# A macaron network of four layers on one core: grouped projections with joined weights, paired tiles and paired key chunks, and a later load of the second group

## What is computed

```python
def global_latent_attn(x, wq, w_kv_down, w_k_up, w_v_up, wo):
    q = split_heads(x @ wq, H)
    latent = x @ w_kv_down
    k = split_heads(latent @ w_k_up, KVH)
    v = split_heads(latent @ w_v_up, KVH)
    q, k = (rope(q, BASE_G), rope(k, BASE_G))
    q, k = (qk_norm(q), qk_norm(k))
    ...
x = x + global_latent_attn(rmsnorm(x, norm1_w), g_wq, g_kv_down, g_k_up, g_v_up, g_wo)
x = x + local_gqa_attn(rmsnorm(x, norm2_w), l_wq, l_wk, l_wv, l_wo)
```

## Time and profile before

| | us |
|---|---|
| median of 3 runs (1966.89 to 1970.33) | 1969.22 |
| the profiled execution | 1968.03 |
| its span, first to last instruction | 1966.3 |
| TensorE busy in it (86%) | 1696.1 |
| VectorE busy (49%) | 954.9 |
| ScalarE busy (41%) | 814.5 |

### The profile page before, as it was taken

One profiled execution on the slowest core, in us unless ns is written; L12 is line 12 of the kernel. 1 busy time (PEld: TensorE's weight loads), 2 busy tenths in 40 slices (PEclk: granted clock), 3 DMA queues, 4 the chain that ended last, 5 costly groups with the idle time before them and its releaser, 6 DMA issues. The chain is left out here.

```text
span 1966.3 us, 25234 instructions
## 1 busy us (share of the span) xinstructions
PE 1696.1 (86%) x8834; PEld 911.8 (46%) x8882; DVE 954.9 (49%) x2236; ACT 814.5 (41%) x1325; POOL 306.1 (16%) x443
## 2 busy tenths in 40 slices
PE   7688896499998988799889999999869985789998
PEld 2334564244443556344444454666623333454665
DVE  5755236687775333511351013445643348774445
ACT  5354133256667323222132124221378864654221
POOL 1102322122233423100210004000100001014000
PEclk9888998699999899899989999999679996889999
DMA  3623104400100310000000002553231103403553
GB/s 81 255 60 133 53 22 104 119 26 26 50 26 2 143 45 28 16 0 0 1 0 0 0 21 66 132 116 83 47 89 31 31 4 81 125 30 78 120 127 86
DMA packets 55383, 120.90 MB, mean 61 GB/s; under 512 B 7767, under 2 KB 34007, under 8 KB 50467
## 3 DMA queue, kind: packets, MB, share of 16 engines
q1 hardware_dynamic: 52796, 114.31, 21.9%
q0 software_dynamic: 2432, 5.00, 0.8%
q10 hardware_dynamic: 39, 0.07, 0.0%
HBM read 86.14 MB, written 19.96 MB: 54 GB/s over the span
## 5 line engine op out<-in xcount | busy, mean ns | idle before, releaser
L970 PE MATMUL psum<-f_h,w 128*128 128x512 f32 (+1 forms) x512 | 223.4, 594 | 8.6 <-ACT f_h L941 6.2
L1754 DVE TENSOR_REDUCE a_most<-psum 128x1 f32<-128x512 f32 (+3 forms) x304 | 182.0, 656 | 46.2 <-PE psum L1604 34.2
L1716 ACT ACTIVATE a_probs<-psum 128x512 f32<-128x512 f32 (+1 forms) x304 | 155.3, 578 | 94.8 <-PE psum L1634 62.6
L2550 ACT ACTIVATE t_silu<-psum 128x512 f32<-128x512 f32 x136 | 81.2, 597 | 241.1 <-PE psum L2608 240.0
L2625 PEld LDWEIGHTS psum<-t_slot,t_hid 128*128 128x128 f32 x1024 | 132.0, 191 | 55.9 <-issue 49.7
L970 PEld LDWEIGHTS psum<-f_h,w 128*128 128x128 f32 x512 | 96.0, 190 | 131.7 <-issue 118.9
L2002 ACT ACTIVATE ga_probs<-psum 128x1024 f32<-128x1024 f32 (+2 forms) x160 | 138.3, 952 | 23.6 <-PE psum L1918 23.4
L2721 DVE TENSOR_TENSOR t_prod<-t_silu,psum 128x512 f32<-128x512 f32 x104 | 71.6, 688 | 137.4 <-ACT t_silu L2550 137.4
L2625 PE MATMUL psum<-t_slot,t_hid 128*128 128x128 f32 x1024 | 134.5, 276 | 2.9 <-DVE t_hid L2712 2.9
L2608 PE MATMUL psum<-xnT,t_slot 128*128 128x512 f32 x256 | 131.5, 595 | 3.1 <-ACT t_silu L2550 3.1
L2613 PE MATMUL psum<-xnT,t_slot 128*128 128x512 f32 x256 | 130.7, 592 | 0.0
(11 more groups left out here) (379 smaller groups left out, 2859.1 us busy)
## 6 DMA issues: line engine op xcount, KB each, us to landing
t_spread<-factors SPq DMA_DIRECT2D x64, 512.0 KB, 6.4
m_experts<-experts_dram SPq DMA_DIRECT2D x14, 768.0 KB, 10.3
c_halves<-xnT SPq DMA_DIRECT2D x48, 128.0 KB, 2.3
t_slot<-experts_dram SPq DMA_DIRECT2D x32, 192.0 KB, 5.3
a_qs<-scratch_q SPq DMA_DIRECT2D x16, 288.0 KB
a_ks<-scratch_k SPq DMA_DIRECT2D x24, 192.0 KB
ga_qs<-scratch_q SPq DMA_DIRECT2D x16, 288.0 KB
la_qs<-scratch_q SPq DMA_DIRECT2D x16, 288.0 KB
```

The lines of the kernel that those rows point to most:

```text
L970: ins = pe.matmul(core.psum[:, HID[n % 2], :], w(name, i * HT + j), src, start=(i == 0), stop=(i == HT - 1))
L1716: act.activation(probs[:, (n * BLOCKS + b) % PROBS, h0:h0 + heads, 0:wide], src, ACT.Exp, scale=SCALE).then_inc(probs_ready, 1)
L1754: v.tensor_reduce(most[:, row, h0:h0 + heads, qt % KPH], src, AX.X, ALU.max).then_inc(max_read, 1)
```

## The change

- `Split` counts queries and keys with semaphores of their own. With `pair=2` (kinds "g" and "l") keys are cut into parts once for two chunks: the even chunk's keys are turned to PSUM rows 0 to 31, the odd chunk's to rows 32 to 63, by a matmul with the identity at a tile position, and the three copies and two subtractions of the keys run on 64 rows after the odd chunk alone; two DMAs store them.
- "g": the compressing weights are turned and multiplied by the up weights once, on TensorE, and ScalarE copies query weights and products into one 128 x 352 tile `joined`. `down` and `compressed` go; a tile's projection is one matmul, as in "l".
- ScalarE writes the cosines and sines out for all tiles at the start of the stage (`turn_by`, `table`). A product instruction then covers two tiles and both tables, 128 x 640 out of two PSUM banks. ScalarE copies the values of two tiles at a time.
- `project(0)` moves ahead of the turning of chunks 2 and 3. `heads` holds all chunks.
- The squares are written head by head, so that the head sums read adjacent elements. The Newton step has three instructions.
- `ahead` is 1 in all three attentions: group 1 is loaded in the attention stage.

```diff
-        for i, transfers in enumerate((self.PARTS, 1)):
-            for odd in range(2):
-                sp.wait_ge(self.spilled[i][odd], 16 * transfers * chunks // 2)
+        for odd in range(2):
+            sp.wait_ge(self.spilled[0][odd], 16 * self.PARTS * chunks // 2)
+            steps = (chunks // self.pair + 1 - odd) // 2
+            if steps:
+                sp.wait_ge(self.spilled[1][odd], 16 * self.pair * steps)
...
+        step, odd = divmod(c, self.pair)
+        if odd == self.pair - 1:
+            sp.wait_ge(self.part_ready[1], self.parted(step, self.PARTS - 1))
+            rows = self.rows[1] // self.pair
+            for k in range(self.pair):
+                b, at = divmod((step * self.pair + k) * CH, T)
+                dst = self.scratch[1][:, b, :, at:at + CH].rearrange("p r t -> r p t")
+                sp.dma_start(dst, self.parts[1][k * rows:(k + 1) * rows, :, step % 2, :]).then_inc(self.spilled[1][step % 2], 16)
...
+            if kind == "g":
+                pe.transpose(core.psum[0:LATENT, DOWN_BANK, 0:P], w("g_down"), core.c("ident")).then_inc(down_pe, 1)
+                pe.wait_ge(down_ready, 1)
+                a = L3_COLS["g_k"][0]
+                pe.matmul(core.psum[:, UP_BANK, 0:3 * VW], down_turned[:, :], w5[0:LATENT, a:a + 3 * VW], start=True, stop=True).then_inc(up_pe, 1)
 
             def project(c):
+                pe.wait_ge(ln.xnT_ready, c + 1)
                 for t in range(TPC * c, TPC * (c + 1)):
                     if t >= TPC:
-                        pe.wait_ge(cos_step, 2 * (t - TPC + 1))
-                        pe.wait_ge(v_ready, t - TPC + 1)
...
+                        pe.wait_ge(turned_by, (t - TPC) // 2 + 1)
+                        pe.wait_ge(v_ready, (t - TPC) // 2 + 1)
+                    pe.matmul(core.psum[:, QKV_BANK[t % TPC], 0:WIDE], core.xnT[:, t * P:(t + 1) * P], weights, start=True, stop=True).then_inc(qkv_pe, 1)
...
+                for t in range(TPC):
+                    ins = pe.matmul(core.psum[rows, T_BANK[1], t * P:(t + 1) * P], heads[:, c, t, D:QK], core.c("ident"), start=True, stop=True, tile_position=(0, odd * VW))
+                if odd == PAIR - 1:
+                    ins.then_inc(sp_.heads_pe[1], 1)
 
             ln.tensor(pe, 0)
             ln.tensor(pe, 1)
-            down(0)
+            if kind == "g":
+                pe.wait_ge(joined_ready, 4)
+            project(0)
             ln.tensor(pe, 2)
-            down(1)
             ln.tensor(pe, 3)
-            project(0)
-            down(2)
-            down(3)
             project(1)
...
+            act.activation(turn_by[:, :, :, :].rearrange("p f k (d h) -> p (f k d) h", h=GROUP), by_tile, ACT.Copy).then_inc(turn_by_ready, 1)
+            act.wait_ge(turn_by_ready, 1)
+            for f in range(2):
+                dst = table[:, :, f, :].rearrange("p k (g r) -> p k g r", r=HD * GROUP)
+                act.activation(dst, turn_by[:, f, :, :].unsqueeze(2).broadcast_to([P, TILES, HN // GROUP, HD * GROUP]), ACT.Copy).then_inc(table_ready, 1)
...
-                act.activation(square[:, :, :], heads[:, c % 2, :, :], ACT.Square).then_inc(squared, 1)
+                dst = square[:, :, :, :].rearrange("p t (g h) d -> p (t g) d h", h=GROUP)
+                act.activation(dst, heads[:, c, :, :].rearrange("p t (g d h) -> p (t g) d h", d=HD, h=GROUP), ACT.Square).then_inc(squared, 1)
...
+                v.tensor_tensor(both[:, 2 * k:2 * k + 2, :, :].rearrange("p t f q -> p t (f q)"), core.psum[:, bank:bank + 2, 0:2 * QK],
+                                table[:, at:at + 2, :, :].rearrange("p t f q -> p t (f q)"), ALU.mult).then_inc(turned_by, 1)
...
-                s.chain(v.tensor_reduce(per_head(mean[:, :, :]), by_head(square[:, :, :]), AX.X, ALU.add))
+                s.chain(v.tensor_reduce(mean[:, :, :], square[:, :, :, :], AX.X, ALU.add))
...
-            stacks = Stacks(core, actx, "a1_", sems["a1_"], scratch, (P, P), [GROUP, T], 3, 2)
+            stacks = Stacks(core, actx, "a1_", sems["a1_"], scratch, (P, P), [GROUP, T], 3, 1)
...
-                stacks = Stacks(core, actx, tag, sems[tag], scratch3, (P, 4 * HD), [T], ring, 2)
+                stacks = Stacks(core, actx, tag, sems[tag], scratch3, (P, 2 * 4 * HD), [T], ring, 1, pair=2)
```

240 lines of the change are left out of this document (109 added, 131 removed).

## The result

The changed kernel took 1944.17 us (median of 4 runs, 1938.66 to 1948.27) beside 1969.78 for the kernel before on the same chip: ratio 0.9875, 95% interval 0.9853 to 0.9897. On another chip it took 1940.07 beside 1971.87, ratio 0.9846 (0.9813 to 0.9880). The gain is 25 to 32 us. The forecast was 1937 with a range of 1928 to 1948.

What follows compares the result with a forecast made beforehand. It took TensorE to set the pace in the global projection, VectorE in the local one, with SyncE late at each projection's end. Gains by stage, less load costs, summed to 32.5 us off 1969.2: forecast 1937, range 1928 to 1948.

Steps and rivals of the forecast that it cites:

- second layer, projection's end: Second layer's projection: without group 1's load, chunk 3's parts are issued earlier; gain 7 us, bounds 5 and 9.
- The walk over the two projections: Global and local projections: stepping through four engines' lists gave rounds of 23.7 us (global) and 22.1 us (local).
- most of it lies under the head of the stage: Guarded attention: group 1's moved load costs between 0 and 5.0 us, taken as 1 because the stage's head covers most.
- the loads come late: Rival: second layer's first maxima wait the full 5 us, band attention's second group 3; 1943.5 us, chance 0.06.
- The start of the global projection: Global projection, stage start to first head sum: 22.4 us before, first head sums at +16.5 after; gain 5.9 us.
- TensorE's clock in the rounds: Projection rounds: the clock falls back to half, so `project(3)` takes 5 us and delays `turn(1)`, parts and squares.
- two rivals: TensorE at half clock all through, 1945.8 us, chance 0.14; TensorE keeping full clock, 1928 us, chance 0.07.
- The squares: ScalarE's strided writes in the projections: unknown cost, 0 to 0.55 us eight times, 0 to 2.7 us by the walk.
- the third rival: Stride penalty moves from head sums to squares, at 1.27 us: 1939.7 us, or 1944 if sums stay slow; chance 0.10.
- Two tiles in one instruction: VectorE in the projection rounds: two products of 640 elements at 0.75 us, 1.50 a round instead of 1.88.
- The moved loads elsewhere: Last part to next stage: gain 0.4 us global, 3.5 local; band attention cost 0.5, at worst 3.
- TensorE's wait for the first maxima: Sign in the new trace, guarded attention: this wait would be 3 to 5 us, against 3.2 before.

Runs made afterwards that it cites:

- early load: Changed kernel with the second layer's second load put back in its projection: 1940.17 us, ratio 0.9835 to the kernel before.
- maxima-first: Changed kernel with the first half's first maxima issued between the loads of groups 1 and 2 in the guarded attention: 1932.54 us, ratio 0.9812.
- loads alone: Kernel before with only the second group's load of all three attentions moved from the projection into the attention: 1968.29 us, ratio 0.9980.

## Why the prediction was right, and where it was not

Term by term, gains in us, from the two traces of the changed kernel:

| term | forecast | measured |
|---|---|---|
| second layer, projection's end | 7 | 6.3, 4.6 |
| second layer, load in the attention | -1 | -6.8, -5.5 |
| global: to the first head sum | 5.9 | 8.5, 8.5 |
| global: three rounds | 10.4 | 9.4, 9.4 |
| global: to the last part, to the next stage | 2.5 | 2.0, 2.0 |
| local: to the first head sum | 1.9 | 2.2, 2.2 |
| local: three rounds | 2.3 | 2.4, 2.4 |
| local: to the last part, to the next stage | 4.0 | 4.0, 3.8 |
| band attention | -0.5 | 0.8, 1.0 |
| sum | 32.5 | 28.7, 28.4 |

The walk over the two projections was sound, and the second layer was not: 6 us of gain were forecast there, and -0.5 and -0.9 measured. The total lies in the range because that miss is partly made up by the global start and the band attention, and because the range was wide enough for it.

**The step that failed** is "most of it lies under the head of the stage", the price of 1 us for group 1's load in the guarded attention. I weighed the bytes against the 5.0 us that the load had occupied SyncE's list, which was only a time of issuing, and took the bound for the whole risk. It cost 5.3 to 7.8 us in the six traces that have two loads ahead of the maxima, past the bound of 5. The early load and the maxima-first runs showed the mechanism: behind two loads TensorE goes on 9 to 11 us after the maxima's issue, behind one 3.2, and the DMA engines are busy meanwhile. The rival "the loads come late" named this wait and was half right: TensorE's wait grew by 5.4 to 7.8 us, but the band attention lost nothing. A late transfer is to be read from its landing, in rows of TensorE's waits, not from the length of SPq rows. The projection's own 7 was high as well: chunk 3's three issues of queries, put at the 3.10 us of the earlier trace rows, took 4.8 to 6.2 with no load ahead of them.

**The start of the global projection** gained 2.6 us more. I had `project(0)` begin 7.1 us into the stage and take 5 us, at half clock; it began at 6.2 and took 3.57, since the clock came up within it, and `project(1)` took 2.60. The joined weights and the moved `project(0)` did all of that gain (13.7 us to the first head sum with them). The rounds were 1.0 longer than forecast. The forecast had counted on cheap squares and cheap sums together, and neither layout gives both; that this is the whole 1.0 is argued, not shown.

**TensorE's clock in the rounds** went neither rival's way, and it did not matter. The forecast let `project(3)` take 5 us and hold back `turn(1)`, the parts and the squares, and two rivals took their times from the same path. In the local projection chunk 3's four tiles took 2.60 us in the changed kernel and 4.29 in maxima first, same code:

```profile
1632.77 2.60 PE L2823 MATMUL psum<-w,xnT 128*128 128x352 f32 x8 [2.06 <-ACT l_v_all L2863]
```

```profile
1614.62 4.29 PE L2826 MATMUL psum<-w,xnT 128*128 128x352 f32 x8 [2.05 <-ACT l_v_all L2866]
```

Their rounds took 22.09 and 22.07 us. So this projection is not what the rounds wait for. That the local rounds came out at 22.1 as forecast is luck: two errors cancel, a slow projection that costs nothing and squares that took 1.33 us where 0.72 was counted. The clock matters at the stage's start, where the forecast for the local projection met traces with the late rise.

**The squares.** I took the lower end, no cost, on the ground that ScalarE idles ahead of them. The penalty was there in full, 1.33 for 0.73, and the third rival's 1.27 was the better guess of the instruction. But it is no loss to the kernel: writing them flat again gains nothing, because the head sums then pay. By the Trainium skill's rule on SBUF cachelines, in "Advanced Engine Details and Errata", section "SBUF Cachelines", the new 32-byte stride had to pay. The trace agrees with it, as it did for the sums' 16 bytes.

**Two tiles in one instruction** was in the rounds at 0.38 us each (1.88 against 1.50), 1.1 in three. It measured 0.6 in the three rounds of either stage, and gave 0.3 of that back at the global start. The saving on VectorE is real (0.2 us for four products), but the round is a chain over two engines, VectorE waits in it, and half of the saving is lost.

**The moved loads elsewhere.** The last stretch of the local projection fell from 5.6 to 2.2 us, as forecast, but the loads alone take 2.0 us off the end, where 3.5 were given to them: chunk 3's three issues of queries need 4.07 us even with nothing ahead of them. The keys cut in pairs and the head sums do the rest (0.8 and 0.7 at the end when undone). The band attention gained 0.8 to 1.1 rather than losing 0.5.

**Two slips in its numbers.** The window that it calls the second round of the global projection runs from 15.7 to 29.2 us into the stage, over the end of the start and most of the first round; the second round is 1406.04 to 1419.68. The reading stands there too: TensorE is busy 12.68 of 13.64 us, at 0.50. And the parts of VectorE's new round add up to 6.6 and 7.8 us, not 6.7 and 7.9.

Of the tests that the prediction named, these held: the projections' lengths (52.5 and 50.7 forecast, 51.6 and 50.5 measured), the pitch of the 640-element products (0.73 against 0.75), and the squares at 1.27, the upper of the two values named (1.33). The guarded attention began 6.3 us earlier in one trace and 4.6 in the other, where 6 to 8 was asked. The head sums' successor began 0.84 us after them and not 0.76. TensorE's wait for the first maxima, 11.05 against 3 to 5, failed.

## What to carry to other kernels

A load moved out of a crowded stage must be followed to the small transfer that is issued behind it in its new place: order the queue by who is waited for first, not by what can be issued first. Cut the work of the engine that is full (here TensorE's compressed path, with `project(0)` moved 15.8 of 19.9 us) before polishing the engines beside it; an instruction saved on an engine that waits for another later in the same round gives a fraction of its time. An edit that moves a stride from the reader to the writer can move its cost as well. Compare traces by stretches between two events of the same code, not by stage totals: here the start of one stage moved by 1.7 us with the clock, which a total mixes with what the edits did, while the rounds behind it repeated within 0.03 us.
